# Cross-attention and mixture of experts: low parts of the expert weights one slice a step, last logits in another bank, second group written out

## The reference

```python
x = x + attention(layernorm(x), ctx, ctx, mask, Wq, Wk, Wv, Wo)   # scores scaled by sqrt(8)
flat = layernorm(x)
logits = flat @ router_w.T
topk_scores, topk_idx = top_k(logits + router_bias, 2)
combine[n, topk_idx] += softmax(topk_scores)
hidden = silu(flat @ gate_proj) * (flat @ up_proj)                # for each expert
out = sum over experts of combine * (hidden @ down_proj)
out = out + (silu(flat @ sh_gate.T) * (flat @ sh_up.T)) @ sh_down.T
x = x + out
```

## Time and profile before

| What | us |
|---|---|
| median of 3 runs | 191.14 (190.18 to 191.35) |
| profiled execution | 192.16 |
| its span, first to last instruction | 190.4 |
| TensorE busy | 171.7 (90%) |
| VectorE busy | 162.8 (86%) |
| ScalarE busy | 123.9 (65%) |
| GpSimd busy | 78.6 (41%) |
| mean granted clock of TensorE | 0.982 |

### The profile page before, as it was taken

One profiled execution on the slowest core, in us unless ns is written; L12 is line 12 of the kernel. 1 busy time (PEld: TensorE's weight loads), 2 busy tenths in 40 slices (PEclk: granted clock), 3 DMA queues, 4 the chain that ended last, 5 costly groups with the idle time before them and its releaser, 6 DMA issues.

```text
span 190.4 us, 4431 instructions
## 1 busy us (share of the span) xinstructions
PE 171.7 (90%) x1512; PEld 134.0 (70%) x1512; DVE 162.8 (86%) x444; ACT 123.9 (65%) x282; POOL 78.6 (41%) x138
## 2 busy tenths in 40 slices
PE   7786599899999999979998659999999999999962
PEld 7664456676787877767776538778788888888841
DVE  5899999689999999979929955887999799979981
ACT  2294375678999999979978434456555656565641
POOL 5745791617776677975697571200000000000000
PEclk9999969999999999999999996999999999999999
DMA  5998600000000000005200221242455347325601
GB/s 126 302 254 211 270 6 3 2 3 0 5 0 3 2 3 0 3 17 155 64 0 9 97 75 51 74 98 100 141 150 122 90 125 158 122 81 132 115 0 55
DMA packets 13060, 15.36 MB, mean 81 GB/s; under 512 B 1521, under 2 KB 8049, under 8 KB 12913
## 3 DMA queue, kind: packets, MB, share of 16 engines
q1 hardware_dynamic: 12608, 14.57, 27.0%
q10 hardware_dynamic: 432, 0.55, 1.3%
HBM read 13.93 MB, written 1.18 MB: 79 GB/s over the span
## 4 chain that ended last, share of the span: by engine, by line
PE 45%; DVE 28%; POOL 6%; ACT 6%; issue 5%; DVEq 0%; ACTq 0%
PE bank L1089 30%; DVE prob L802 7%; DVE smax L800 6%; PE bank L1042 4%; POOL w_lo L461 3%; DVE xn L705 2%; DVE hid L878 2%; PE bank L975 2%; ACT hid_hi L638 2%; DVE cmix_sb L878 1%; DVE hid_lo L870 1%; PE bank L1028 1%; DVE att L791 1%; DVE inv_den L789 1%; DVE top_i L779 1%
## 5 line engine op out<-in xcount | busy, mean ns | idle before, releaser
L629 ACT ACTIVATE sig<-bank 128x512 f32<-128x512 f32 x36 | 21.5, 600 | 23.5 <-PE bank L1089 23.0
L1089 PE MATMUL bank<-xt_hi,w_hi 128*128 (+1 forms) x72 | 30.0, 416 | 0.1
L1089 PE MATMUL bank<-xt_lo,w_hi 128*128 (+1 forms) x72 | 28.6, 397 | 0.0
L1089 PE MATMUL bank<-xt_hi,w_lo 128*128 (+1 forms) x72 | 28.4, 395 | 0.0
L861 DVE TENSOR_TENSOR hid_u<-sig,bank 128x512 f32<-128x512 f32 x32 | 21.8, 682 | 4.9 <-PE bank L1089 3.4
L802 DVE TENSOR_TENSOR prob<-bank,smax 128x512 f32<-128x512 f32 x32 | 22.1, 692 | 1.1
L800 DVE TENSOR_REDUCE smax<-bank 128x8 f32<-128x512 f32 x32 | 21.8, 681 | 1.0 <-PE bank L1042 1.0
L565 ACT COPY prob_t<-bank 128x512 f32<-128x512 f32 x32 | 17.3, 588 | 6.6 <-PE bank L1018 6.4
L570 ACT ACTIVATE prob<-prob 128x512 f32<-128x512 f32 x32 | 20.0, 629 | 1.8 <-DVE prob L802 1.1
L1042 PE MATMUL bank<-k_blk,q_blk 64*128 64x256 f32 x128 | 18.1, 402 | 2.1 <-ACT comb_t L642 1.0
L870 DVE TENSOR_TENSOR hid_lo<-hid,hid_hi 128x512 fp32r<-128x512 f32 x24 | 17.3, 723 | 1.3 <-ACT hid_hi L638 0.6
(11 more groups left out here) (112 smaller groups left out, 381.1 us busy)
## 6 DMA issues: line engine op xcount, KB each, us to landing
mix_all<-w_rows SPq DMA_DIRECT2D x64, 128.0 KB, 3.0
w_moe_sb<-w_moe SPq DMA_DIRECT2D x1, 1728.0 KB, 10.3
x_sb<-x SPq DMA_DIRECT2D x4, 256.0 KB, 7.1
ctxt_sb<-ctx_t SPq DMA_DIRECT2D x4, 256.0 KB, 5.9
ctx_sb<-ctx_nat SPq DMA_DIRECT2D x4, 256.0 KB, 5.1
out<-x_sb SPq DMA_DIRECT2D x3, 256.0 KB, 2.3
w_att_sb<-w_att ACTq DMA_DIRECT2D x1, 272.0 KB, 6.0
mrow<-mask_row ACTq DMA_DIRECT2D x1, 256.0 KB, 4.7
```

Source lines behind the costliest of these rows:

```text
L629: nc.scalar.activation(sig[r][:, :], gate_ps[r][:, :], ACT.Silu).then_inc(s_sig, 1)
L1089: last = nc.tensor.matmul(out, w, moving, start=start and k == 0, stop=stop and k == 2)
```

## The change

GpSimd makes the low parts of the weights in slices of 216 columns, `low_weights(t-1)` in step t between `q_block` and `norm2`, and the last slice behind the steps; gates of group 0 wait for the slices they read. The last four tiles' logits are written to bank 1. In the change-over routers, normalizations, transposed attention and VectorE's indices are moved, most of them to a later unit. The wait for the copy of the first weight rows moves from the end of step 11 to step 12. Units of the second group are written out, so that the last expert weights are transposed in slot (1, 2) instead of (0, 8). SP stores them at pair 14 instead of 12. ScalarE's copy of the tokens of tiles 13 to 15 waits for a low part two tiles back.

```diff
...
+        last_logit_ps = banks[1][:, 0:EXPERTS]
...
-            for m in range(first, UNITS):
-                slot(0, m)
-            with eng.Fori(0, GROUPS - 1) as i:
+            for n in range(first, 2 * UNITS):
+                slot(n // UNITS, n % UNITS)
+            with eng.Fori(0, GROUPS - 2) as i:
                 for m in range(UNITS):
-                    slot(i + 1, m)
+                    slot(i + 2, m)
...
-                if n == EPAIRS + SPREADS:
+                if n == 2 * EPAIRS - 2:
                     store_rows(2)
+                if n == 2 * EPAIRS:
                     sp.wait_ge(s_w_rows, 48)
                 spread_weights(n)
...
-            def low_weights(u):
-                cols = slice(u * W_UNIT, (u + 1) * W_UNIT)
-                pool.wait_ge(s_w_hi, min(TILES, -(-(u + 1) * W_UNIT // W_STEP)))
+            def low_weights(t):
+                cols = slice(t * W_STEP, (t + 1) * W_STEP)
+                pool.wait_ge(s_w_hi, t + 1)
                 nc.gpsimd.tensor_tensor(w_lo[:, cols], w_moe_sb[:, cols], w_hi[:, cols].bitcast(F32),
                                         ALU.subtract).then_inc(s_w_lo, 1)
...
             def step(t, p, on):
                 if on(-2):
                     q_block(t + 2, p, first=False)
+                if on(1):
+                    low_weights(t - 1)
                 if on(2):
                     norm2(t - 2, p)
                 if on(-2):
                     k_blocks(t + 2, p)
-                elif t == TILES - 2:
-                    for u in range(3):
-                        low_weights(u)
-                elif t == TILES - 1:
-                    for u in range(3, 5):
-                        low_weights(u)
                 if on(4):
                     low_tokens(t - 4, p)
...
             norm2(TILES - 2, 0)
             low_tokens(TILES - 4, 0)
-            low_weights(5)
-            low_weights(6)
+            low_weights(TILES - 1)
             low_tokens(TILES - 3, 1)
-            low_weights(7)
-            low_weights(8)
+            low_tokens(TILES - 2, 0)
             norm2(TILES - 1, 1)
-            low_tokens(TILES - 2, 0)
             low_tokens(TILES - 1, 1)
...
             def tokens_to_sbuf(t, p):
                 act.wait_ge(s_xt2, t + 1)
+                if t > TILES - GT:
+                    act.wait_ge(s_xt2_lo, t - 1)
...
-                if isinstance(g, int) and (g, m) == (0, UNITS - 1):
+                if isinstance(g, int) and (g, m) == (1, 0):
+                    tanh_of(2)
+                if isinstance(g, int) and (g, m) == (1, 2):
                     weights_to_sbuf(2)
...
             transposed(t, p, 1)
             attention_to_sbuf(t - 1, 1 - p)
             silu(0, 0)
+            values_to_sbuf(t)
             silu(0, 1)
             high_weights(t)
-            values_to_sbuf(t)
             high_part(0, 1)
             tokens_to_sbuf(t - 3, 1 - p)
             weights_to_sbuf(1)
+            slot(0, 2)
             normalized(t - 2, p)
-            slot(0, 2)
-            normalized(t - 1, 1 - p)
             slot(0, 3)
             attention_to_sbuf(t, p)
             tokens_to_sbuf(t - 2, p)
+            normalized(t - 1, 1 - p)
             slot(0, 4)
-            normalized(t, p)
             tokens_to_sbuf(t - 1, 1 - p)
             slot(0, 5)
+            normalized(t, p)
+            slot(0, 6)
             tokens_to_sbuf(t, p)
-            slot(0, 6)
-            tanh_of(2)
...
             t, p = TILES - 1, (TILES - 1) % 2
             product(0, 0)
             residual(t - 1, 1 - p)
-            largest(t - 4)
             moments2(t - 1, 1 - p)
-            largest_index(t - 4, p)
             mean_and_variance(t - 1, 1 - p)
             product(0, 1)
             low_part(0, 1)
             weighted(0, 1)
+            largest(t - 4)
+            largest_index(t - 4, p)
             attention(t, p)
             slot(0, 2)
+            slot(0, 3)
             largest(t - 3)
             largest_index(t - 3, 1 - p)
-            slot(0, 3)
+            slot(0, 4)
             residual(t, p)
             largest(t - 2)
             moments2(t, p)
             largest_index(t - 2, p)
             mean_and_variance(t, p)
-            slot(0, 4)
+            slot(0, 5)
             largest(t - 1)
             largest_index(t - 1, 1 - p)
-            slot(0, 5)
+            slot(0, 6)
+            slot(0, 7)
             largest(t)
             largest_index(t, p)
-            slot(0, 6)
+            slot(0, 8)
+            slot(1, 0)
             top_two(2)
             two_weights(2)
-            expert_slots(dve, slot, 7)
...
             def attention_transposed(t, p):
                 pe.wait_ge(s_att, t + 1)
+                if t >= TILES - 2:
+                    pe.wait_ge(s_top_i, t - 3)
                 if t > 0:
                     pe.wait_ge(s_x1, t)
                 nc.tensor.transpose(at_ps, att[p][:, :, :].rearrange("p h d -> p (h d)"), ident_sb).then_inc(s_at, 1)
...
-            def router(t, p, summed):
+            def logits(out, t, p):
+                nc.tensor.matmul(out, ones_sb[:, :], bias_row_sb, start=True, stop=False)
+                nc.tensor.matmul(out, xt2[p][:, :], wr_sb, start=False, stop=True).then_inc(s_logit, 1)
+            def router(t, p):
                 pe.wait_ge(s_xt2_hi, t + 1)
-                pe.wait_ge(s_x1, summed)
+                pe.wait_ge(s_x1, t + 3 if t < TILES - GT - 1 else TILES - 1)
                 if t > 0:
                     pe.wait_ge(s_top_i, t)
-                nc.tensor.matmul(logit_ps, ones_sb[:, :], bias_row_sb, start=True, stop=False)
-                nc.tensor.matmul(logit_ps, xt2[p][:, :], wr_sb, start=False, stop=True).then_inc(s_logit, 1)
+                logits(logit_ps, t, p)
+            def last_router(t, p):
+                pe.wait_ge(s_xt2_hi, t + 1)
+                pe.wait_ge(s_att, TILES)
+                pe.wait_ge(s_top_i, t)
+                logits(last_logit_ps, t, p)
...
-                    router(t - 4, p, t - 1)
+                    router(t - 4, p)
                 if t == 2 * GT + 3:
                     weights_as_rows(0)
+                if t == 2 * GT + 4:
+                    pe.wait_ge(s_ct_sb, 1)
                 if on(3):
                     norm_transposed(t - 3, q)
...
-                if t == 2 * GT + 3:
-                    pe.wait_ge(s_ct_sb, 1)
...
-                if isinstance(g, int):
-                    pe.wait_ge(s_w_lo, m + 1)
+                if isinstance(g, int) and g == 0:
+                    pe.wait_ge(s_w_lo, -(-(m + 1) * W_UNIT // W_STEP))
...
-                if isinstance(g, int) and (g, m) == (0, UNITS - 1):
-                    pe.wait_ge(s_top_i, TILES)
+                if isinstance(g, int) and (g, m) == (1, 2):
                     weights_as_rows(2)
...
             gate(0, 0)
             transposes(t, p, 0)
             values_as_rows(t - 1)
+            transposes(t, p, 1)
             pe.wait_ge(s_sub[1], TILES)
             up(0, 0)
-            router(t - 4, p, t - 1)
-            transposes(t, p, 1)
+            attention_transposed(t - 1, 1 - p)
             weights_as_rows(1)
             norm_transposed(t - 3, 1 - p)
-            attention_transposed(t - 1, 1 - p)
             pe.wait_ge(s_pt_sb[0], TILES)
             gate(0, 1)
+            output_projection(t - 1, 1 - p)
             values(t, p)
             up(0, 1)
-            output_projection(t - 1, 1 - p)
             gate(0, 2)
+            router(t - 4, p)
+            values_as_rows(t)
             up(0, 2)
-            values_as_rows(t)
             down(0, 2)
             gate(0, 3)
-            router(t - 3, 1 - p, t)
+            attention_transposed(t, p)
             up(0, 3)
+            last_router(t - 3, 1 - p)
             pe.wait_ge(s_ct_sb, 2)
             norm_transposed(t - 2, p)
-            pe.wait_ge(s_top_i, t - 2)
-            attention_transposed(t, p)
             down(0, 3)
             gate(0, 4)
-            router(t - 2, p, t)
             output_projection(t, p)
             up(0, 4)
+            last_router(t - 2, p)
             norm_transposed(t - 1, 1 - p)
             down(0, 4)
             gate(0, 5)
-            router(t - 1, 1 - p, TILES)
             up(0, 5)
-            norm_transposed(t, p)
+            last_router(t - 1, 1 - p)
             down(0, 5)
             gate(0, 6)
-            router(t, p, TILES)
             up(0, 6)
+            norm_transposed(t, p)
             down(0, 6)
-            expert_slots(pe, slot, 7)
+            gate(0, 7)
+            up(0, 7)
+            last_router(t, p)
+            down(0, 7)
+            expert_slots(pe, slot, 8)
...
```

8 lines of the change are left out of this document (5 added, 3 removed).

## The result

The changed kernel takes 189.42 us (median of 12 runs, 188.8 to 190.14). The kernel before takes 191.19 beside it (12 runs, 190.18 to 193.44). The ratio is 0.9924 with a 95% interval of 0.9898 to 0.9949: 0.76% faster, where 1.5% was forecast (188.2). It lies inside the range of 185.0 to 191.2, but the forecast step of 2.9 us came out as 1.8.

A forecast was written before the change was run, and what follows sets the result against it. Bounds: VectorE and a two-step path without slack in the attention steps, TensorE's waits in the change-over, TensorE in the expert units. 2.9 - 5.8 = -2.9 took the profiled execution to 189.3, the median to 188.2; range 185.0 to 191.2.

The forecast's parts named there:

- the forecast step of 2.9 us: Whole kernel: attention steps 2.9 us later and change-over 5.8 gained, summing to -2.9.
- the last of the sum: From profiled execution to median: 192.16 becomes 189.3, and being 1.02 above the median 191.14, gives a median of 188.2.
- the 4.3 of the waits: Change-over: three TensorE waits go (0.95 + 1.46 + 2.24 = 4.65), with 0.35 of the 6.15 total left for short waits.
- The low weights in every step, +2.9: Attention steps: GpSimd's subtraction waits for ScalarE's cast, norm 0.71 later, double step 8.59 for 7.88; 2.9 us later.
- the wait at 81.99: Attention steps: TensorE's 0.99 us wait for the copy of the weight rows goes by moving one step later.
- The change-over, -5.8: Stage between attention steps and expert units: three TensorE waits and the slow clock behind them go, 5.8 us gained.
- no wait on TensorE over 0.1 us: Change-over in its new order: estimated arrival times leave TensorE no wait above 0.1 us.
- VectorE's first product: Change-over: it waited 3.72 us until 100.18 and was forecast to come at about 99.3.
- The second group written out: Expert units: same instructions without the loop's turn, put at nothing since the loop shows no gap.
- The subtraction was not hidden: Rival, attention steps: subtraction fits GpSimd's idle 0.77 us, only the wait at 81.99 goes, 184.5 us; chance 0.11.
- The waits did not move: Rival, change-over: TensorE's waits only move to new places, half the gain (3.0), 191.0 us; chance 0.18.
- TensorE's clock did not fall in the attention steps: Rival: TensorE idling 0.35 us each attention step lowers its clock; three such steps give 193.9 us; chance 0.08.

## Why the prediction was right in its parts, and where it failed

*The step that failed is the last of the sum:* "It lies 1.02 above the median 191.14, so the median becomes 188.2." It takes the distance between one execution and the median for a constant that the change leaves alone. It isn't. The profiled execution (span 190.4) has the slow stretch of the change-over. The median (span 189.3) stands at the upper edge of the executions that by their spans don't have it. So the 1.02 is for the most part this very stretch, and its removal was already in the sum with 1.5: it was subtracted twice. The profiled execution of after is at its own median (189.42).

What the stretch is worth to the median is on record: filling the wait took it away and lowered the median by 0.7, not by 1.5. The other term that was mis-sized is the attention steps, 3.3 and not 2.9. With the 4.3 of the waits as forecast, that makes 3.3 - 4.3 - 0.7 = -1.7; measured is -1.8. The means agree: -1.0 in every execution, and 1.5 less in 36 of 82, is -1.7, and the mean fell from 191.31 (the 82) to 189.48 (the twelve). In executions at full clock -1.0 should be left: 190.27 before, and 189.24 in the only one of the changed kernel at 1.000. One execution is little to go by (the next, at 0.995, took 188.80).

*The low weights in every step, +2.9:* right by its mechanism, too small by 0.4. The norm starts 0.60 us after the subtraction, as I had taken it (its own length is 0.645 on the mean), the norm was 0.73 late for 0.71, and the double step was 8.61 for 8.59. The residual at 97.94 for 97.8 looks better than it is, as the steps began 0.3 sooner. Nor does the loop run at 8.6 throughout: of the 3.3 us, 2.8 are lost by the residual at 72.09 (26.9 us from 45.15, where before it was 69.58 - 45.45 = 24.1), where the forecast has 1.9, and only 0.5 in the six steps behind it (25.85 instead of 25.33), where it has 0.9. That the loss comes from the cast and not from the work is shown by moving the subtraction one step. The sentence that the wait at 81.99 "moves to the next step, where the copy is long done, and goes" is right alone (0.8 to 0.9), and in the changed kernel its gain was used up by 0.39 of lateness and 0.4 of contention.

*The change-over, -5.8:* right in the profiled execution, 5.8. One detail was wrong: "no wait on TensorE over 0.1 us" met one of 0.67 for the index of tile 12 and one of 0.24. And of VectorE's first product, forecast at 99.3 in the clock of before, came 102.62 - 3.03 = 99.6.

*"The second group written out: the same instructions without the loop's turn", at nothing:* right as a cost, but it hid what it is for. Without it, the last weights' transposition holds TensorE for 3.29 us.

*The rivals.* The subtraction was not hidden. The waits did not move, though 0.91 of them stayed. TensorE's clock did not fall in the attention steps: waits of 0.27 to 0.77 us in eleven of them, 4.7 in all, left it at 1.00 from 36.8 to 97.5. So what the Trainium skill says of short and frequent idling (TensorE: Matmul & The Clock Gate, A second HAM failure mode), which I weighed there, did not show in this kernel. Two readings of this rival were wrong. TensorE did have gaps in the steps before, two of 0.26 and 0.20 us for k_blk. And the clock did not fall after the wait of 1.46, only after that of 2.24; it had also fallen once ahead of the steps, at 23 to 27 us. From the trace of before:

```profile
22.76 0.66 PE L956 MATMUL bank<-consts_sb,xn 128*128 128x128 f32 x4 [2.08 <-DVE xn L705]
```

```profile
107.50:112.00 4.50, 4.50 (x23) 3.50 (x23) 3.81 (x15) 1.89 (x6) 3.49 (x4) 1.00 0.32 115
```

## What to carry to other kernels

Before you subtract a profiled execution's distance from the median, ask what in it makes the distance. If the same thing is a term of the sum, it is counted twice, and it pays only in the executions that have it. The span and mean clock of every execution show this where a single trace can't: look whether they fall into groups, and at which group's edge the median stands. And a piece of work that seems to fit an engine's idle time fits only if its input is there when that time begins; one step later may be free (3.94 us a step instead of 4.3 here).

## What the runs showed that I had not expected

The same waits of 0.95, 1.46 and 2.24 us are in every trace of before, but by the mean clock a third of the executions has no slow stretch, and by the spans some 46 of 82 lack the one of the change-over. An early wait of 2.08 us was followed by a low clock in the traces of before and not in two traces of later versions. A slow stretch can be kept away by products nobody reads: eight of them, 1.98 us, took the granted clock behind the wait from 0.51 to 1.00 and moved nothing else. And where the clock fell behind a wait, it cost much more than its length: some 6 us for 3.29, and 6.4 to 6.8 for 1.62 + 2.45.

The best versions measured are not the changed kernel but the change without its dealing of the low weights (186.84), with the dealing a step later (186.97), and with two steps spared (186.62). They don't differ by more than the runs can tell. The dealing itself is worth having only with its input ready: as it stands in the change it costs 4.2 us in the steps and gives 1.5 in the change-over.
